# A four-layer graph network on one core: a slot between the attention stage's handshakes, and filter stage and scatter in one block

## The reference

```python
# L0 attention, 8 heads of 16
alpha = sum_d(q[dst] * (k[src] + e)) / sqrt(d);  m = segment_max(alpha, dst)
ex = exp(alpha - m[dst]);  w = ex / segment_sum(ex, dst)[dst]
agg = segment_sum(w * (v[src] + e), dst);  out = LN((agg + skip) @ Wo + bo + x)
# L1 edge MLP
messages = relu([x[src], x[dst], edge_attr32] @ W1.T + b1) @ W2.T + b2
y = x + relu(segment_sum(messages, dst) @ Wu.T + bu)
# L2 filter
W = ssp(edge_attr50 @ w0.T + b0) @ w2.T + b2;  c = 0.5 * (cos(edge_weight / 10 * pi) + 1)
agg = segment_sum(c * (W * h1[src]), dst);  y = ssp((h1 + agg) @ lin2.T + b) @ lin.T + b
# L3 gated: mean over incoming and over outgoing edges, then a GRU cell
a_in = segment_mean((h @ W_in.T + b_in)[src], dst);  a_out = segment_mean((h @ W_out.T + b_out)[dst], src)
h = gru_cell(concat(a_in, a_out), h)
```

## Time and profile before

| | |
|---|---|
| median of three runs | 6,061.47 us (6,058.81 to 6,064.39) |
| the profiled execution, its own time | 6,069.15 us |
| its span in the trace | 6,067.4 us |
| busy, PE / DVE / ACT / POOL | 64% / 60% / 46% / 71% of the span |
| mean DMA rate | 107 GB/s |
| granted TensorE clock, mean | 0.776 |

### The profile page before, as it was taken

The page is one execution under the profiler, slowest core; times in us unless marked ns, Lnnn a source line. Parts: engine busy times, 40 slices in busy tenths (PEclk is TensorE's granted clock), DMA queues, the critical chain, the costliest instruction groups (busy, mean ns, idle before and its releaser), DMA issues. The chain is left out here.

```text
span 6067.4 us, 93501 instructions
## 1 busy us (share of the span) xinstructions
PE 3864.7 (64%) x20652; PEld 3150.3 (52%) x20652; DVE 3646.7 (60%) x11761; ACT 2805.5 (46%) x6913; POOL 4300.4 (71%) x4477
## 2 busy tenths in 40 slices
PE   5567667765776777678887885344343446666665
PEld 5566666654555555455565554333333346665444
DVE  6788888886988888667777674101011034445665
ACT  3788888883211111155655553111111158884444
POOL 2676777663777777767777776677777777777775
PEclk8787888786999888878889887555555579998877
DMA  4444444453755555622323224322222245553223
GB/s 124 121 135 127 129 127 125 127 118 91 202 147 149 145 147 150 127 66 74 74 74 74 74 74 62 101 77 77 76 75 75 72 119 164 165 166 85 57 58 46
DMA packets 485365, 649.30 MB, mean 107 GB/s; under 512 B 120187, under 2 KB 332938, under 8 KB 484822
## 3 DMA queue, kind: packets, MB, share of 16 engines
q0 software_dynamic: 155552, 345.75, 22.9%
q1 hardware_dynamic: 329271, 297.58, 18.1%
HBM read 495.44 MB, written 150.71 MB: 106 GB/s over the span
## 5 line engine op out<-in xcount | busy, mean ns | idle before, releaser
L694 POOL DMA_INDIRECT kv_ring<-keys_values,gather_i x880 | 857.6, 975 | 376.3 <-issue 247.1
L2112 POOL DMA_INDIRECT rows_by_src<-arena,key x880 | 869.1, 988 | 309.6 <-issue 258.6
L694 POOL DMA_INDIRECT arena<-table,gather_i x880 | 856.7, 973 | 278.8 <-issue 266.7
L694 POOL DMA_INDIRECT e_ring<-filter_rows,gather_i x880 | 839.3, 954 | 300.0 <-issue 267.3
L694 POOL DMA_INDIRECT e_ring<-table,gather_i x880 | 845.5, 961 | 275.5 <-issue 264.5
L2096 PE MATMUL rs_ph<-nodes,arena 128*128 x1664 | 424.2, 436 | 667.2 <-ACT arena L2105 615.3
L2096 PEld LDWEIGHTS rs_ph<-nodes,arena 128*128 128x128 f32 x1664 | 365.6, 324 | 726.2 <-issue 726.0
L2088 DVE TENSOR_SCALAR arena<-arena,part 128x512 f32<-128x512 bf16 x220 | 112.6, 514 | 949.3 <-PE rs_ph L2096 899.2
L2338 PE MATMUL gl_sum_f<-arena,gl_hot_f 128*128 128x128 f32 x1760 | 291.9, 317 | 433.7 <-DMA arena<-table,gather_i 212.6
L1566 PE MATMUL e_pa<-e_msg,e_hot 128*128 128x128 f32 x3520 | 542.0, 304 | 31.4 <-DVE e_msg L1769 24.7
L743 DVE TENSOR_TENSOR arena<-arena,e_pa 128x128 f32 x1760 | 497.3, 283 | 99.9 <-PE e_pa L1566 69.6
(11 more groups left out here) (460 smaller groups left out, 9798.0 us busy)
## 6 DMA issues: line engine op xcount, KB each, us to landing
rows_by_src<-e_filler SPq DMA_DIRECT2D x256, 260.0 KB
arena<-rows_by_src SPq DMA_DIRECT2D x256, 260.0 KB, 3.0
at_rows<-local_rows SPq DMA_DIRECT2D x220, 128.0 KB
e_rows<-local_rows SPq DMA_DIRECT2D x220, 128.0 KB
arena<-local_rows SPq DMA_DIRECT2D x220, 128.0 KB
e_attr<-edge_attr SPq DMA_DIRECT2D x880, 25.0 KB
kv_ring<-keys_values,gather_i POOLq DMA_INDIRECT x880
e_ring<-table,gather_i POOLq DMA_INDIRECT x880
```

Of the source, the lines that this page charges most:

```text
L694: pool.indirect_dma_start(ring[:, r, u, :], None, table, bass.IndirectOffsetOnAxis(index, 0)).then_inc(arrived[r], 16)
L2112: pool.indirect_dma_start(self.table, bass.IndirectOffsetOnAxis(place, 0), self.out[:, r, u, :], None, bounds_check=SLOTS_R - 1, oob_is_er ...
```

## The change

**Attention.** `LAG` goes from 8 to 9 and `NODE_AT` one more beyond that. Each link of the chain is put into a slot, or a half of a slot, of its own: what one engine makes in a slot the next engine reads in the following one. On PE `total` now runs ahead of the transpositions, one slot later than its messages, and `return_max` moves into the next chunk's phase 0. On ACT `carries`, `inverse_root` and `exponents` are moved from the end of a slot to places ahead of `keep_values`. On DVE `add` lags one slot more, and `shift`, `scan_runs` and `walk` stand behind `products`. `rank_one` writes into a free part of the bank of `pa` and no longer into that of the transpositions. SP loads the penalties with the last batch of a chunk, not with the first.

```diff
-LAG = 8
+LAG = 9
-NODE_AT = [BUCKET_ENDS[n] + LAG + 1 for n in range(NB)]
+NODE_AT = [BUCKET_ENDS[n] + LAG + 2 for n in range(NB)]
@@ stage_attention, SP
-                if k % CB == 0:
+                if k % CB == CB - 1:          # loads the penalties
@@ PE: turn_scores, rank_one
-                at_least(pe, rescaled, n, None)
+                at_least(pe, shifted, n, None)
+                at_least(pe, fallen, 3 * n, None)
...
+                at_least(pe, added, U * (n * CB - 1) + 2, None)
+                pe.matmul(outer, lhs, fac[0:1, :], start=True, stop=False)
@@ PE, one slot
                 node_sums(s)
+                km = s - LAG - 1
+                if 0 <= km < BATCHES:
+                    if km % CB == 0:
+                        rank_one(km // CB)
+                    total(km)
                 if ph == 1 and 0 <= n < CHUNKS: turn_scores(n)
                 if ph == 2 and 0 <= n < CHUNKS: turn_runs(n)
+                if ph == 3 and 0 <= n < CHUNKS:
                     turn_carries(n)
-                if ph == 3 and 0 <= n < CHUNKS:
-                    return_max(n)
                 if ph == 0 and 0 <= n - 1 < CHUNKS:
-                    rank_one(n - 1)
-                if 0 <= s - LAG < BATCHES:
-                    total(s - LAG)
+                    return_max(n - 1)
@@ ACT, one slot (after)
+                edge_hot(s - LAG - 1)
+                if ph == 0: carries(n - 1)
                 turned_hot(s + 1)
+                inverse_root(...)
+                if ph == 1: exponents(n - 1)
                 keep_values(s - 1); exps(s - LAG); spreads(n) if ph == 1
-                if ph == 2: carries(n)
-                if ph == 3: exponents(n)
@@ DVE
                 dve.wait_ge(ranked, n + 1)
+                dve.wait_ge(summed, 2 * n * CB + 1)
@@ DVE, one slot (after)
+                products(s - 1); shift(n - 1) if ph == 1; scan_runs(n) if ph == 2; walk(n) if ph == 3
+                rescale(ka); add(ka, 0); head_sums(s - 2); add(ka, 1)
+                scan_all(n - 1) if ph == 0; score(n) if ph == 1
+                add(ka, 2); weigh(km); add(ka, 3); message(km); ...node steps...
```

```diff
@@ stage_edges, POOL
             if layer == 2:
-                for k in range(EARLY):
+                for k in range(BATCHES):
                     c.by_source.scatter(pool, k)
+                pool.wait_ge(c.by_source.tabled, 16)
+                gather_rows(pool, c, c.table, c.by_source.ring_f, c.by_source.arrived_f, [], range(FR))
+                for r in range(R):
+                    pool.wait_ge(c.by_source.scattered[r], 16 * U * BATCHES // R)
@@ SP
+                if layer == 2 and PRE_ROWS <= k < PRE_ROWS + PRE:
+                    sp.wait_ge(numbered, 18)
+                    c.by_source.load(sp, k - PRE_ROWS)
...
+    def rest_of_sync(self, sp, renewed):
+        for to, of in self.loads:
+            sp.dma_start(to, of).then_inc(self.loaded, 16)
+        for k in range(PRE, BATCHES):
+            self.load(sp, k)
+            if k == EARLY + 2 * R:
+                sp.wait_ge(renewed, NB)
+                sp.dma_start(self.c.table3.rearrange("t p f -> p t f"), self.c.x[:, :, :]).then_inc(self.tabled, 16)
@@ ACT copy_soft, PE turn_soft
+                if PRE_AT <= n < PRE_AT + PRE * U:
...
+                    c.by_source.pack_tile(act, n - PRE_AT, pn[:, 0, 2 * P:3 * P])
...
+                    pe.wait_ge(renewed, PRE * U)
+                    c.by_source.rows_of_tile(pe, n - PRE_AT, pn[:, 0, 2 * P:3 * P])
@@ RowsBySource.scatter
-            pool.indirect_dma_start(self.table, bass.IndirectOffsetOnAxis(place, 0), self.out[:, r, u, :], None,
-                                    bounds_check=SLOTS_R - 1, oob_is_err=False).then_inc(self.scattered[r], 16)
+            pool.indirect_dma_start(self.table, bass.IndirectOffsetOnAxis(place, 0), self.out[:, r, u, :], None)\
+                .then_inc(self.scattered[r], 16)
+PRE = 4
+EARLY = 12
+EARLY_AT = {BATCHES + 2 + b - PRE: b for b in range(PRE, EARLY - 1)} | {BATCHES + 13: EARLY - 1}
+PRE_ROWS, PRE_HOTS, PRE_AT, PARTS_READY = 100, 112, 30, 13
@@ stage_gated, POOL
-            gather_rows(pool, c, c.table, ring_f, arrived_f, [(summed_f, 1)])
+            gather_rows(pool, c, c.table, ring_f, arrived_f, [(summed_f, 1)], range(FR, BATCHES))
```

More of the change, by code:

```diff
@@ L1078, in _ @@
                     turned_hot(0)
-                if 0 <= s - LAG < BATCHES:
-                    edge_hot(s - LAG)
+                if 0 <= s - LAG - 1 < BATCHES:
+                    edge_hot(s - LAG - 1)
+                if ph == 0 and 0 <= n - 1 < CHUNKS:
+                    carries(n - 1)
                 if s + 1 < BATCHES:
                     turned_hot(s + 1)
+                for lag, w in ((FIRST, 0), (SECOND, 1)):
+                    if node_due(s, lag + 1) is not None:
+                        inverse_root(node_due(s, lag + 1), w)
+                if ph == 1 and 0 <= n - 1 < CHUNKS:
+                    exponents(n - 1)
                 if 0 <= s - 1 < BATCHES:
@@ L1259, in _ @@
                 ph, n = phase(s)
-                chain = 0 <= n < CHUNKS
-                ka, km = s - LAG - 1, s - LAG
+                ka, km = s - LAG - 2, s - LAG
                 adding = 0 <= ka < BATCHES
                 which = loaded_values(nc, c.bucket_d, ka, DVE_ENGINE, NT - 1) if adding else None
-                if chain and ph == 2:
-                    scan_runs(n)
-                if chain and ph == 3:
-                    scan_all(n)
                 if 0 <= s - 1 < BATCHES:
                     products(s - 1)
+                if ph == 1 and 0 <= n - 1 < CHUNKS:
+                    shift(n - 1)
+                if ph == 2 and 0 <= n < CHUNKS:
+                    scan_runs(n)
+                if ph == 3 and 0 <= n < CHUNKS:
+                    walk(n)
                 if adding and ka % CB == 0:
@@ L1277, in _ @@
                     add(ka, 1, which[1])
-                if chain and ph == 1:
+                if ph == 0 and 0 <= n - 1 < CHUNKS:
+                    scan_all(n - 1)
+                if ph == 1 and 0 <= n < CHUNKS:
                     score(n)
-                if chain and ph == 2:
-                    walk(n)
-                if chain and ph == 3:
-                    shift(n)
+                if adding:
+                    add(ka, 2, which[2])
                 if 0 <= km < BATCHES:
@@ L1414, in _ @@
             if layer == 2:
-                sp.wait_ge(numbered, 16)
-                for k in range(EARLY):
-                    c.by_source.load(sp, k)
+                c.by_source.rest_of_sync(sp, renewed)
             if layer == 1:
@@ L1531, in _ @@
                 2: [(6, copy_sums), (13, copy_soft), (1, softplus), (8, soften_nodes), (15, last_root), (14, pack_early)]}[layer])
+            if layer == 2:
+                for k in range(EARLY, BATCHES):
+                    c.by_source.pack(act, k, pt)
         @block.tensor
@@ L2067, with __init__ @@
 class RowsBySource:
-    def __init__(self, nc, c):
+    def __init__(self, nc, c, loads, p_in, p_out, gate_rows):
         sem = lambda n: c.semaphore("rs_" + n)
+        self.loads, self.p_in, self.p_out, self.gate_rows = loads, p_in, p_out, gate_rows
+        self.biases = arena(c, ACC0, [3, 4 * F])[0:1, :, :]
+        self.parts = arena(c, ACC0 + 12 * F, [9, 4 * F], BF16)[0:1, :, :].rearrange("one (p b) n -> one p b n", b=3)
+        self.loaded, self.tabled, self.made, self.took, self.kept, self.tiled = (sem(n) for n in ("loaded", "tabled", "made", "took", "kept", "tiled"))
+        self.ring_f = arena(c, QUERY0 + RR * U * REV, [FR, U, F])
+        self.arrived_f = [sem(f"arrived_f{r}") for r in range(FR)]
         self.nc, self.c = nc, c
@@ L2105, in pack, with rows_of_tile @@
         act.activation(self.out[:, r, :, 0:F], ph[:, k % 2, :, :], ACT.Copy).then_inc(self.packed, 1)
+    def rows_of_tile(self, pe, e, to):
+        which = self.nc.values_load_multi_w_load_instructions(
+            self.c.bucket_d[:, e:e + 1], engines=(PE_ENGINE,), min_val=0, max_val=NT - 1,
+            skip_runtime_bounds_check_because="the vector engine made them within these bounds")[1][0]
+        pe.wait_ge(self.hots_t, e // U + 1)
+        at_least(pe, self.tiled, tiled_by(e), None)
+        ins = pe.matmul(to, self.hot_t[:, e // U, e % U, :], of_bucket(self.c.x, which), start=True, stop=True)
+        if e % U == U - 1:
+            ins.then_inc(self.ready, 1)
@@ L2204, with tiled_by @@
+def tiled_by(e):
+    return 0 if e <= 0 else min(e, PRE * U) + -(-min(e, PRE * U) // U)
 RR = 8
```

264 lines of the change are left out of this document (121 added, 143 removed).

## The result

The changed kernel takes 6,020.73 us (median of four runs, 6,009.66 to 6,025.79), the kernel before 6,060.26 us beside it; the ratio is 0.9928, 95% interval 0.9916 to 0.9941. That is faster by 0.7%, 40 us, and outside the range of 5,900 to 5,985 us.

The account below looks back on a forecast made before the run. The prediction took POOL's five streams of 880 indirect transfers to set the time. Attention -62, filter to scatter -40.5, no index bound -33 and early gathers +11.6 gave -124 us from 6,061.5: 5,937, rounded to 5,935 (range 5,900 to 5,985).

## What to carry to other kernels

Before a waiting engine is given earlier data, sum up all that fills its time, "issue" included: a wait that is taken away only pays as far as nothing else on that engine moves into its place. In this kernel a register load cost up to 0.54 us where the instruction ahead of it was short and nothing behind one of 0.69 us, so try it behind the longest instruction of a slot. And a transfer that is moved ahead of a barrier takes its cover with it: ask what ran beside it.

## What the runs showed of the hardware

- A load of four bucket numbers holds DVE's sequencer for 352 ns in the median (205 loads in attention, 341 to 601). Behind a step of 0.18 us up to 0.54 us of it are seen as idle time of DVE; behind an instruction of 0.69 us it is hidden.
- An indirect scatter of 128 rows takes 969 ns without and 983 ns with an index bound, and 969 ns with rows of 512 B as with 520 B; a gather takes 944 ns with rows of 512 B (medians of 880).
- Two DVE adds of which the second waits for the first by a semaphore have 0.21 us between them (102 places, 21.5 us); with `weigh` in between the entry is gone.
